# A fused retention and feed-forward layer whose batch loop is written out: no loops and no registers

## What is computed

```python
xn = layernorm(x)                                   # (8, 512, 128)
q, k, v = heads(xn @ Wq), heads(xn @ Wk), heads(xn @ Wv)
for each chunk:                                     # state S per head
    attn = (q @ k.T) * D                            # D: causal decay within the chunk
    o    = attn @ v + (q * decay_q) @ S
    S    = decay_s * S + (k * decay_k).T @ v
h   = bitlinear(xn, w_fc) + gate * (xn @ v_.T @ fast_b.T @ u.T)
out = x + o @ Wo + bitlinear(max(h, 0)**2, w_proj)
```

## Time and profile before

| | us |
|---|---|
| median of 3 runs | 143.44 |
| lowest, highest | 142.6, 146.62 |
| the profiled execution | 142.48 |
| its span, first to last instruction | 140.6 |

### The profile page before, as it was taken

The page is one execution under the profiler, slowest core; times in us unless marked ns, Lnnn a source line. Parts: engine busy times, 40 slices in busy tenths (PEclk is TensorE's granted clock), DMA queues, the critical chain, the costliest instruction groups (busy, mean ns, idle before and its releaser), DMA issues.

```text
span 140.6 us, 6479 instructions
## 1 busy us (share of the span) xinstructions
PE 121.4 (86%) x2809; PEld 93.7 (67%) x2809; DVE 89.4 (64%) x255; ACT 76.3 (54%) x152; POOL 52.8 (38%) x52
## 2 busy tenths in 40 slices
PE   0557996799999999859999999999999999996750
PEld 0125974598779777747779787878787878763530
DVE  0676375777768967854378958885888588017402
ACT  2140549754785677407574777377738772783010
POOL 8139913550355046400364055305530643067000
PEclk9999999599999999995999999999999999999999
DMA  4948500012201250124001420150013002301001
GB/s 104 354 114 378 219 5 2 0 37 50 71 5 30 51 154 0 41 57 135 0 0 37 130 57 0 47 153 24 0 47 103 0 0 48 101 5 75 5 5 75
DMA packets 5005, 9.55 MB, mean 68 GB/s; under 512 B 1264, under 2 KB 1520, under 8 KB 4864
## 3 DMA queue, kind: packets, MB, share of 16 engines
q1 hardware_dynamic: 4528, 8.72, 20.2%
q10 hardware_dynamic: 464, 0.63, 1.3%
HBM read 5.42 MB, written 2.10 MB: 53 GB/s over the span
## 4 chain that ended last, share of the span: by engine, by line
PE 79%; ACT 6%; DVE 4%; issue 4%; DMA 3%; POOL 1%; POOLq 1%
PE ps_work L572 11%; PE ps_score L640 10%; PE ps_work L574 8%; PE ps_work L573 8%; PE ps_score L613 6%; PE ps_y L667 5%; PE ps_y L671 5%; PE ps_score L652 5%; PE ps_y L668 5%; PE ps_score L628 3%; DMA x_in<-x_tok 3%; PE ps_turn L579 3%; ACT square L322 2%; ACT sq_hi L331 1%; ACT square L327 1%
## 5 line engine op out<-in xcount | busy, mean ns | idle before, releaser
L290 POOL TENSOR_TENSOR sq_lo<-square,sq_hi 128x512 fp32r<-128x512 f32 x32 | 41.0, 1283 | 70.8 <-ACT sq_hi L331 70.8
L322 ACT ACTIVATE square<-ps_work 128x512 f32<-128x512 f32 x32 | 19.1, 597 | 26.7 <-PE ps_work L574 26.0
L455 DVE TENSOR_TENSOR scores<-ps_score,cst 128x512 f32<-128x512 f32 x32 | 20.5, 681 | 6.2 <-PE ps_score L613 6.2
L331 ACT ACTIVATE sq_hi<-square 128x512 fp32r<-128x512 f32 x32 | 19.9, 624 | 0.0
L327 ACT ACTIVATE square<-square 128x512 f32<-128x512 f32 x32 | 18.5, 627 | 0.0
L640 PE MATMUL ps_score<-scores,v_pad 64*32 64x64 f32 x1024 | 15.0, 227 | 3.8 <-issue 3.8
L640 PEld LDWEIGHTS ps_score<-scores,v_pad 64*32 64x32 f32 x1024 | 12.7, 104 | 4.9 <-issue 4.1
L430 DVE TENSOR_SCALAR xn<-x_in,mean_var,rstd 128x128 f32<-128x128 f32 x32 | 15.2, 538 | 0.3
L572 PE MATMUL ps_work<-xn_hi,w_hi 128*128 128x512 f32 x32 | 14.5, 454 | 0.4 <-issue 0.4
L667 PE MATMUL ps_y<-sq_hi,w 128*128 128x512 f32 x32 | 13.5, 422 | 1.3 <-DVE resid L478 1.0
L436 DVE TENSOR_TENSOR xn_lo<-ps_turn,xn_hi 128x512 fp32r<-128x512 f32 x8 | 5.5, 693 | 13.6 <-ACT xn_hi L309 13.6
(11 more groups left out here) (90 smaller groups left out, 216.4 us busy)
## 6 DMA issues: line engine op xcount, KB each, us to landing
x_in<-x_tok SPq DMA_DIRECT2D x8, 256.0 KB, 3.5
resid<-x_feat SPq DMA_DIRECT2D x1, 2048.0 KB, 7.6
out_feat<-resid SPq DMA_DIRECT2D x8, 256.0 KB, 2.3
q_pair<-q_dec SPq DMA_DIRECT2D x56, 32.0 KB, 2.0
po_in<-ffn_weights SPq DMA_DIRECT2D x1, 320.0 KB, 5.2
fc_in<-ffn_weights SPq DMA_DIRECT2D x1, 256.0 KB, 4.3
q_table<-q_decay ACTq DMA_DIRECT2D x1, 256.0 KB, 6.3
wqvk<-qvk_weights ACTq DMA_DIRECT2D x1, 192.0 KB, 5.4
```

The costliest lines, as they stand in the source:

```text
L290: nc.gpsimd.tensor_tensor(sq_lo[p][:, f, :], square[p][:, f, :], sq_hi[p][:, f, :].bitcast(F32), ALU.subtract).then_inc(lo_ready, 1)
L322: nc.scalar.activation(square[b.parity][:, f, :], ps_work[f % 2][:], ACT.Relu).then_inc(relu_ready, 1)
L331: nc.scalar.activation(sq_hi[b.parity][:, f, :], square[b.parity][:, f, :], ACT.Copy).then_inc(hi_ready, 1)
L455: nc.vector.tensor_tensor(scores[:, g].rearrange("p t s i -> p (t s) i"), ps_score[:, g].rearrange("p (a i) -> p a i", i=BLK), causal.unsq ...
```

## The change

The batch number becomes a Python integer. All engines' programs are written out for the eight batches, the loops and all register computations go, and all waits compare with constants. The two waits on `zeroed` in TensorE's `gather_states` and `carry` go as well (VectorE's wait on it stays). Order and work of every engine are otherwise the same.

```diff
 class Batch:
-    def __init__(self, half, offset):
-        self.half, self.offset = half, offset
-        self.index, self.parity = half * 2 + offset, offset % 2
+    def __init__(self, index):
+        self.index, self.parity = index, index % 2

     def step(self, k):
-        return Batch(self.half, self.offset + k)
+        return Batch(self.index + k)

-def over_batches(engine, body):
-    body(Batch(0, 0), False, True)
-    with engine.Fori(0, NB // 2 - 1) as half:
-        body(Batch(half, 1), True, True)
-        body(Batch(half, 2), True, True)
-    body(Batch(NB // 2 - 1, 1), True, False)
+def over_batches(body):
+    for index in range(NB):
+        body(Batch(index), index > 0, index + 1 < NB)
...
-                return x_tok[:, bass.ds(index * SEQ, SEQ)].rearrange("p (t d) -> p t d", d=D)
+                return x_tok[:, index * SEQ:(index + 1) * SEQ].rearrange("p (t d) -> p t d", d=D)
...
-                cols = bass.ds(b.index * SEQ, SEQ)
+                cols = slice(b.index * SEQ, (b.index + 1) * SEQ)
...
-            body(first, False, True, True)
-            with sync.Fori(0, 2) as half:
-                body(Batch(half, 1), True, True, True)
-                body(Batch(half, 2), True, True, True)
-            body(Batch(2, 1), True, True, True)
-            body(Batch(2, 2), True, False, True)
-            body(last, True, False, False)
+            for index in range(NB):
+                body(Batch(index), index > 0, index + 2 < NB, index + 1 < NB)
...
-                half = b.half + b.offset // 2
-                dve.wait_ge(x_loaded[b.parity], (half + 1) * 16)
+                dve.wait_ge(x_loaded[b.parity], (b.index // 2 + 1) * 16)
...
             def gather_states(b):
-
-                pe.wait_ge(zeroed, ZEROED)
                 pe.wait_ge(scores_ready, b.count(NG, NG))
...
             def carry(b):
-
-                pe.wait_ge(zeroed, ZEROED)
                 pe.wait_ge(state_ready, b.count(1, 1))
```

More of the change, by code:

```diff
@@ L201, in vk_bank @@
             return (ps_turn if side == 0 else ps_work[0])[:].rearrange("p (w t d) -> p w t d", w=2, t=2)
-        first, last = Batch(0, 0), Batch(NB // 2 - 1, 1)
+        first, last = Batch(0), Batch(NB - 1)
         SPREAD = 16 * H
@@ L291, in body @@
                                             ALU.subtract).then_inc(lo_ready, 1)
-            over_batches(pool, body)
+            over_batches(body)
         @block.scalar
@@ L383, in body @@
                     copy_k_tok(b.step(1), 1)
-            over_batches(act, body)
+            over_batches(body)
             copy_o(last)
@@ L558, in body @@
                     dve.wait_ge(resid_loaded, 16)
-            over_batches(dve, body)
+            over_batches(body)
             take_states(last)
@@ L729, in body @@
                 own_values(b)
-            over_batches(pe, body)
+            over_batches(body)
             carry(last)
```

## The result

The changed kernel took 145.51 us (median of 4 runs, 144.04 to 146.04), the kernel before 143.02 us beside it. The ratio is 1.018 with a 95% interval of 1.012 to 1.024: slower, clear of no change, but whether by more than 2% is open. Ratios here compare the faster executions of both kernels, those within about 1.5% of each kernel's fastest, while medians take all. The profiled execution took 144.04 us with a span of 142.1, 1.56 us over the one of before.

The account below looks back on a forecast made before the run. TensorE was taken as the bound, with instruction fetch stalling its runs of small matmuls. Profiled 142.5 us - 1.2 (registers) + 5.3 (new stalls) - 0.3 (end) + 0.7 (clock) = 147.0 us, range 144.0 to 150.0.

Parts of the forecast that it names:

- the case to which it gave 0.31: Whole kernel: changed time within 2% of the kernel before, chance 0.31.
- the one with 0.63: Whole kernel: changed kernel slower, above the 146.3 us line, chance 0.63.
- Fetch of straight code stalls the dense stretch: TensorE's small matmuls in L628 and L640, 368 instructions, outrun block fetches: new stalls in bodies 3, 5 and 6.
- some 15: TensorE ahead of the first stall: some 15 register and semaphore instructions vanish, which sets where blocks start.
- The place 620: Body 2: a block starts at instruction 620, in L640; the present stall stays, 2.0 to 2.2 us.
- The delay, taken as 3.6 us: TensorE's instruction fetch: the next block is usable 3.6 us after a block is entered, in bodies 3, 5 and 6.
- Body 5, 1.1 us: Body 5, L628 and half of L640: a block lasting 2.4 to 2.5 us gives a new stall of 1.1 us.
- New stalls: Bodies 3, 5 and 6 on TensorE: 2.1, 1.1 and 2.1 us of stall, 5.3 us in all.
- Registers, 1.2 us, all of them TensorE's: TensorE's registers and branches removed: 1.2 us gained; registers of the other engines: nothing.
- The end, 0.3 us gained: Body 7: the second stall comes 12 matmuls into the final L652, not ahead of it: 0.3 us gained, or nothing.
- The clock, 0.7 us more: TensorE's clock: each long stall has an even chance of a low stretch, 0.7 us more, from -1.4 to +2.8.
- The rival built on it: TensorE's straight-line fetch runs far ahead and both old stalls are owed to the loop: 136.4 us, chance 0.05.

Follow-up runs that it names:

- two shifted programs: Changed kernel plus empty semaphore instructions in TensorE's program ahead of its first score, 60 in one, 115 in the other: 147.95 and 151.57 us, one execution each.
- the looped kernels: Kernel before with all engines but TensorE written out, TensorE still looped: 141.45 us, ratio 1.003; repeated 142.62 us, 0.991; also variants with reordered TensorE work or empty instructions.

## Why the prediction was right, and where it was off

Forecast: 147.0 us, 144 to 150, slower. Measured: 145.5 us, slower by 1.8%. The direction and the cause are right, the size is partly luck. The forecast was 4.5 us over the profiled execution and 3.6 over the median of that time; the medians differ by 2.5 us and the profiled pair by 1.6. And 145.5 lies below 146.3, where the prediction itself drew the line of 2%: by that line this is the case to which it gave 0.31 and not the one with 0.63. Its own terms also add up to a somewhat wider range: 142.5 - 2.2 + 4.4 - 0.3 - 0.7 = 143.7 and 142.5 - 0.4 + 5.6 - 0.3 + 3.5 = 150.9. By its steps:

- *Fetch of straight code stalls the dense stretch.* Right, in mechanism and place: bodies 2, 3 and 6 and the final L636, none in bodies 1 and 4, and two shifted programs stalled within a matmul of where the arithmetic put it, in body 0 five or six matmuls early. Blocks of 256 instructions and 699 in a body held to within an instruction or two. The "some 15" that vanish ahead of the first stall did not: the stall of body 2 moved from 51 to 40 remaining matmuls, 22 instructions. By the trace 14 vanish ahead of body 2 and 7 in it. The place 620 was right, but 15 does not lead to it from the earlier trace rows.
- *The delay, taken as 3.6 us.* A little large for two of three. From entering a block to the first instruction of the next it was 3.2 us in body 2, 3.55 in body 3, 3.6 in body 6 (the stall plus the matmuls between): pieces of 1.46, 1.79 and 1.83 us where 2.0 to 2.2 and twice 2.1 stood. Against the earlier trace rows body 2's shrank by 0.5 us. How far one execution carries is seen where TensorE alone was written out: the same three pieces were 1.67, 2.06 and 1.87 us, 5.6 in all and not 5.1.
- *Body 5, 1.1 us.* Wrong: no stall. The step counted the delay from the block's execution, and the packet started 1.5 us ahead of that, where elsewhere it starts about 1 us behind it. The fetch was some 2.5 us sooner, more than the stall forecast. New stalls were 3.6 us, not 5.3, and this term is two thirds of that miss.
- *Registers, 1.2 us, all of them TensorE's.* Too much, and half in the wrong place. With stalls and low clock (1.5 us in body 3 before) taken out, bodies 1 to 6 take 13.58, 13.86, 13.86, 13.58, 13.55 and 13.72 us, against 13.53, 14.07, 13.7, 13.99, 13.84 and 13.72: 0.7 us. It lies in bodies 4 and 5; the differences of bodies 2 and 3, 0.2 us either way, are no larger than what single stalls vary by. The prediction gave the registers of the other engines nothing. In bodies 4 and 5 they were worth as much as TensorE's own, 0.4 of 0.7 us.
- *The end, 0.3 us gained.* About so. The stall of 1.81 us became 0.54 us of waiting for VectorE and 0.91 us of issue; from the start of body 7 to the start of the last addition it took 18.6 us before and 19.9 after, and the low clock of body 7, about 1.5 us, is in that.
- *The clock, 0.7 us more.* Not in the profiled pair: the kernel before had a low stretch behind its first stall and another at 25.3 us in body 0, the changed one only that of body 6. From batch 1's first projection (25.57 us before, 26.22 after) to the start of body 1 the kernel before took 6.88 us and the changed one 5.25; body 1 starts 1.0 us earlier, since 0.65 had been lost ahead of that. Body 3 saves 1.5. This may be why the profiled execution took 144.04 us while the median is 145.51, but it is not shown: the other three executions had a granted clock of 0.955, 0.955 and 0.975 against 0.979, and the one of 0.975 was still 1.9 us longer. Over the profiles of all kernels here 12 of 23 stalls of 1.2 us and more in bodies 0 to 6 brought it, about the even chance assumed.
- *Sum.* Start -1.0, registers -0.7, body 2's stall -0.5, new stalls +3.6, clock in body 3 -1.5, body 7 to the last addition +1.25, behind its start +0.4: 1.5 us, by which the span is longer. The start, and the missing low stretch in body 3, took 2.5 us off this pair, where the prediction had +0.7 for the clock and nothing for the start.

The rule of the Trainium skill in Runtime: NRT & Kernel Launch, section Instruction fetch mechanics, that entering a block is mostly hidden, agrees with 17 of the 21 fetches of the changed kernel, which cost nothing, and not with four, whose fetch began while TensorE ran L614 or L626. The rival built on it (136.4 us) would have needed these four to be hidden as well.

## What to carry to other kernels

Writing a loop out removes registers and branches, here worth 0.7 us, and turns code that stayed on the chip into code that must be fetched, here ten blocks more. Count instructions per microsecond, not per batch: where TensorE ran through a block's 256 instructions in less than about 3.2 to 3.8 us, the next block was late, and only a fetch that had started ahead of the matmuls, among large ones, was spared. Here a loop whose body stays on the chip was worth more than the branch it costs. Slow work inside the dense stretch shortened the stall by 0.6 to 1.0 of its own length; both shifts of the program only moved the stalls elsewhere.

## What the runs showed of the hardware

- The delay had three parts in the recorded stalls: 0.7 to 1.5 us from entering a block to the packet's start (once 0.4), 0.9 to 1.5 us of transfer, and 1.3 to 1.6 us from its end to the next instruction. Together it was 3.2 to 4.0 us, once 2.7. The late fetches of the looped kernels stand apart.
- A loop of some 1420 instructions on TensorE ran its second and third turns with no instruction packet at all.
- A fetch can start ahead of the matmuls: at seven or more crossings among large matmuls the packet started 1.2 to 1.7 us before the block's first matmul.
- A fetch can start late, in four profiles 4.0 to 5.7 us after the block ahead was entered: two programs stalled 2.5 us in one execution at a block that had cost nothing in another.
- A semaphore instruction that waits for nothing took 0.11 us of TensorE's sequencer, against 0.01 us between weight loads in L626.
- A low stretch of TensorE's clock, 3.41 us at 1.2 GHz, added 1.54 us to 11.90 us of work. It followed 12 of 23 stalls of 1.2 us and more in bodies 0 to 6.
